# A rest computed in two halves on GpSimd, each half awaited by TensorE by itself

## The reference, cut to what matters

```python
e = emb_table[feat_index]                      # 512 x 39 x 16
x0 = e
h1 = relu(einsum('bhd,bmd,ohm->bod', x0, x0, conv_w1) + conv_b1)
nxt, hi1 = split(h1, 2, axis=1)                # 64 and 64 rows
h2 = relu(einsum('bhd,bmd,ohm->bod', nxt, x0, conv_w2) + conv_b2)
res = concatenate([hi1, h2], axis=1).sum(axis=2)
y = relu(_bn(flat @ deep_w1 + deep_b1, ...))   # 400 wide, statistics over the batch
y = relu(_bn(y @ deep_w2 + deep_b2, ...))
return concatenate([flat @ linear_w, res, y], axis=1) @ out_w + out_b
```

## Time and profile before

| | us |
|---|---|
| median of 3 runs | 464.21 (463.79 to 464.5) |
| the profiled execution | 464.01 |
| its span, first to last instruction | 462.2 |
| PE busy | 403.8 (87%) |
| DVE busy | 362.8 (79%) |
| POOL busy | 319.2 (69%) |
| ACT busy | 198.2 (43%) |

### The profile page before, as it was taken

The page is one execution under the profiler, slowest core; times in us unless marked ns, Lnnn a source line. Parts: engine busy times, 40 slices in busy tenths (PEclk is TensorE's granted clock), DMA queues, the critical chain, the costliest instruction groups (busy, mean ns, idle before and its releaser), DMA issues. The chain is left out here.

```text
span 462.2 us, 4571 instructions
## 1 busy us (share of the span) xinstructions
PE 403.8 (87%) x1238; PEld 229.4 (50%) x1238; DVE 362.8 (79%) x369; ACT 198.2 (43%) x252; POOL 319.2 (69%) x232
## 2 busy tenths in 40 slices
PE   0001959999999999999999999989999999979996
PEld 0001524554465555556555555546557565655563
DVE  6222658979958888999779777999874988998994
ACT  1104012327432751465156524734564447656443
POOL 5787777775848667886888878832478268729662
PEclk9999988999999999999999999999999999999999
DMA  3756959999998988899999979988957999998910
GB/s 64 146 85 146 152 63 244 238 171 210 221 235 186 226 205 192 191 228 243 237 209 215 219 183 206 232 227 212 220 128 186 236 230 236 241 258 213 237 38 2
DMA packets 41726, 87.95 MB, mean 190 GB/s; under 512 B 15836, under 2 KB 21275, under 8 KB 41700
## 3 DMA queue, kind: packets, MB, share of 16 engines
q1 hardware_dynamic: 28693, 80.48, 70.9%
q0 software_dynamic: 5120, 1.32, 7.9%
q10 hardware_dynamic: 7887, 5.86, 5.4%
HBM read 86.34 MB, written 1.28 MB: 190 GB/s over the span
## 5 line engine op out<-in xcount | busy, mean ns | idle before, releaser
L540 POOL TENSOR_TENSOR zl<-ring,zh 128x1024 fp32r<-128x1024 f32 x60 | 142.5, 2389 | 83.0 <-ACT zh L1022 78.9
L526 POOL DMA_INDIRECT G<-in_emb,idx_all x160 | 161.5, 1010 | 48.2 <-issue 41.7
L662 DVE TENSOR_TENSOR ring<-p_n,ring 128x1024 f32<-128x1024 f32 x147 | 174.0, 1217 | 0.9
L1022 ACT ACTIVATE zh<-ring 128x1024 fp32r<-128x1024 f32 x81 | 85.3, 1056 | 133.3 <-DVE ring L662 130.2
L833 PE MATMUL p_h<-ring,w2s 128*128 128x512 f32 x264 | 124.6, 602 | 6.3 <-DVE ring L662 5.4
L833 PE MATMUL p_n<-placed,w1s 125*128 125x512 f32 (+2 forms) x192 | 92.0, 603 | 0.0
L662 DVE TENSOR_TENSOR placed<-xa,p_x 125x1024 f32<-125x1024 f32 (+2 forms) x45 | 54.7, 1216 | 37.0 <-PE p_x L812 37.0
L833 PEld LDWEIGHTS p_h<-ring,w2s 128*128 128x128 f32 x264 | 50.6, 193 | 56.0 <-issue 44.3
L833 PE MATMUL p_h<-zh,w2l 128*128 128x512 f32 x178 | 68.2, 464 | 1.6 <-DVE zh L625 1.6
L812 PE MATMUL p_x<-stack,put 103*125 103x512 f32 (+3 forms) x116 | 52.5, 534 | 9.7 <-DVE stack L635 9.3
L833 PE MATMUL p_h<-zh,w2h 128*128 128x512 f32 x178 | 56.0, 396 | 0.0
(11 more groups left out here) (113 smaller groups left out, 303.0 us busy)
## 6 DMA issues: line engine op xcount, KB each, us to landing
ring<-xs_scratch SPq DMA_DIRECT2D x294, 256.0 KB, 5.6
xa<-xs_scratch ACTq DMA_DIRECT2D x21, 156.0 KB
G<-in_emb,idx_all POOLq DMA_INDIRECT x160
xs_scratch<-xT ACTq DMA_DIRECT2D x16, 64.0 KB
dw_sb<-in_dw SPq DMA_DIRECT2D x4, 200.0 KB
xa<-xs_scratch SPq DMA_DIRECT2D x3, 156.0 KB
xa<-in_dw ACTq DMA_DIRECT2D x2, 156.2 KB
xa<-xs_scratch ACTq DMA_DIRECT2D x7, 32.0 KB
```

The source lines that it names most:

```text
L526: nc.gpsimd.indirect_dma_start(G[:, b % 2, DIM * f:DIM * (f + 1)], None, emb[:, :], bass.IndirectOffsetOnAxis(idx_all[:, b, f:f + 1], 0)). ...
L540: nc.gpsimd.tensor_tensor(low_of(s), z_of(s), high_of(s).bitcast(F32), ALU.subtract).then_inc(s_low_pool, 1)
L662: nc.vector.tensor_tensor(z_of(s), by, x, ALU.mult).then_inc(s_z, 1)
L1022: nc.scalar.activation(high_of(s), z_of(s), ACT.Copy).then_inc(s_zh, 1)
```

## The change

In GpSimd's `low_part` the one subtraction over 1024 columns becomes two over 512 columns each, and each raises s_low_pool by one. The count that others wait for is therefore doubled (`wait_used`, and TensorE). TensorE waits for the first half ahead of its first matmul on zl, and for the second half ahead of its second. Rests by VectorE stay whole, with one wait.

```diff
@@ wait_used
             elif s in POOL_SPLITS:
-                own_wait(eng, s_low_pool, POOL_SPLITS.index(s) + 1)
+                own_wait(eng, s_low_pool, CHUNKS * (POOL_SPLITS.index(s) + 1))
@@ low_part on GpSimd
                 wait_low_room(pool, s)
                 own_wait(pool, s_zh, SPLITS.index(s) + 1)
-                nc.gpsimd.tensor_tensor(low_of(s), z_of(s), high_of(s).bitcast(F32), ALU.subtract).then_inc(s_low_pool, 1)
+                for c in range(CHUNKS):
+                    half = slice(BANK * c, BANK * (c + 1))
+                    nc.gpsimd.tensor_tensor(low_of(s)[:, half], z_of(s)[:, half], high_of(s)[:, half].bitcast(F32),
+                                            ALU.subtract).then_inc(s_low_pool, 1)
@@ contract on TensorE
-                    rest, count = (s_low_dve, DVE_SPLITS) if s in DVE_SPLITS else (s_low_pool, POOL_SPLITS)
+                    rest, count, parts = (s_low_dve, DVE_SPLITS, 1) if s in DVE_SPLITS else (s_low_pool, POOL_SPLITS, CHUNKS)
...
                         for c in range(CHUNKS):
                             mm(c, wh, high)
-                        pe.wait_ge(rest, count.index(s) + 1)
                         for c in range(CHUNKS):
+                            if c < parts:
+
+                                pe.wait_ge(rest, parts * count.index(s) + c + 1)
                             last = mm(c, wh, low, False, final)
```

## The result

Seven runs of the changed kernel have a median of 462.59 us (461.22 to 464.88), seven of the kernel before on the same chip 464.72 (463.79 to 465.63). The ratio is 0.9954, 95% interval 0.994 to 0.9968: faster by 0.46%, some 2.1 us. Forecast were 459.5 and -4.55 us. The sign was right and the time lies in the range, but the size was more than twice too large.

The account below looks back on a forecast made before the run. TensorE was taken as the bound, so gains could come only from its idle time. Terms of -0.25, -2.2, -1.1 and -1.0 sum to -4.55 us, from 464.01 to 459.5 us, range 458.5 to 463.6.

Parts of the forecast that it names:

- GpSimd's cost: Two halves cost 0.10 us more than one rest, 6.0 us over 60, hidden by GpSimd's 83.0 us of idle time.
- TensorE's 60 new waits: A second wait ahead of each pair's second matmul on zl, if already satisfied, costs 0, at most 0.01 us.
- VectorE is let in between halves: VectorE instructions held by a GpSimd rest go at the boundary between its halves; terms 2 to 4 build on it.
- Rival B: Nothing measurable: VectorE isn't let in between halves of one rest, only the direct halves' gain is left; 463.5 us, chance 0.14.
- C: Slower: the second wait keeps TensorE from loading weights under the first matmul, 0.10 us per rest; 465.5 us, chance 0.06.
- Term 1: TensorE's wait for a rest at 257.39: one matmul instead of two stands behind the last half; -0.25 us.
- Term 2: First normalisation chain: L722 and L732 wait for halves, shortening TensorE's waits at 410.55 and 415.72; -2.2 us.
- L722 goes at 403.53, so L732 is up at 404.53: Term 2's step: L722 goes behind the first half, the three small steps between take 0.95 us.
- Term 3: Block 4: the gather moves behind VectorE's L630, L625 at 299.86 is no longer held, TensorE's 1.18 wait goes; -1.1 us.
- Term 4: Last wait, 450.92: the half brings 0.25 directly and VectorE in front is earlier; -1.0 us, at best all 1.34.
- VectorE gains at least 0.5: Term 4's step: 1.1 gained at the second L732, at worst 0.6 lost at L630 at 428.61.
- Rival A: Only part comes: term 2 or 3 fails, term 4 at its low end; 460.8 or 461.9 us, chance 0.25.

Follow-up runs that it names:

- the small kernel: Computes nothing of the model: 32 stages, VectorE probes beside six GpSimd subtractions of 512 columns; six take 7.36 us with the tiny probe, 8.35 with the two-input one.
- one wait: Changed kernel, but TensorE waits once for both halves ahead of its first matmul on zl; 462.64 us against 464.95 before, ratio 0.9948.
- two rests: Kernel before with only the two GpSimd rests beside the first normalisation chain halved; 463.77 us against 464.95, ratio 0.9978.
- the PSUM version: Kernel before, whole rests, with the results of L722 and L732 written to PSUM instead of SBUF; second run 461.94 us against 465.25, ratio 0.9929.
- Blocks 1 to 4: Kernel before with only the 24 GpSimd rests of blocks 1 to 4 halved; 491.11 us against 491.17 on a slow-loading chip, ratio 0.9994.
- Halves with the exchange: Changed kernel with rest (7,9) moved to GpSimd and (7,11) to VectorE; 491.89 us against 491.17 on a slow-loading chip, ratio 0.9989.
- quarters: Changed kernel with each GpSimd rest in four pieces of 256 columns, TensorE waiting for the second and fourth; 473.01 us against 465.1 before, ratio 1.0178.
- with PSUM: Changed kernel with the results of L722 and L732 in PSUM, run twice; ratios against the kernel before 0.9924 and 0.9917 (460.84 us against 465.25).
- PSUM and the exchange: Changed kernel with L722's and L732's results in PSUM and rests (7,9) and (7,11) exchanged between VectorE and GpSimd; 463.38 us against 465.1 before, ratio 0.9956.

## Why the prediction was right or wrong

- *GpSimd's cost and TensorE's 60 new waits.* Right in size: 0.14 us per rest more (0.10 forecast), and a mean of 400 ns on zl. The cover held only behind block 4: before the change GpSimd had 2.4 us of idle time ahead of the rests between 260 and 306 us, and TensorE had lost 0.57 us by block 4's h2s. The Trainium skill's figure in "GPSIMD Engine Reference", "Performance pitfalls for Q7 kernels", gave an estimate of 0.17 for one more piece, a little nearer than mine. The page states it for a read command; two of them for a subtraction were my assumption. Two sums beside the main one were wrong: with 0.17 the first term is 0.35 - 0.17 = 0.18 and the sum -4.5, not -4.4, and all of terms 3 and 4 makes -4.97, not -5.1.
- *VectorE is let in between halves.* Right for the small steps and for most two-input instructions. Rival B is refuted by L735, let in at 405.91 between the halves of one rest, and by the small kernel; C by the mean on zl.
- **Term 1, -0.25.** Came to nothing (+0.04). One matmul less behind the wait is worth 0.22 (block 3's h2s is at +0.27 with one wait and at +0.05 with two), where I had put 0.35, and the rest itself is 0.25 later (one wait shows 0.56 for it where it was 0.31), by the halves' own 0.14 and what GpSimd has before it. I had taken off only 0.10.
- **Term 2, -2.2: the main miss, measured -1.25.** The step that failed is "L722 goes at 403.53, so L732 is up at 404.53". It left out that the square root between them waits for ScalarE's table load, which ended at 404.35, and it counted 1.55 and 0.84 of TensorE's waits as all VectorE's, while 0.87 of the first was ScalarE's h2s. Phase was bad luck on top and by the estimate above cost little: L725's turn came 0.05 behind a boundary. The second half of the term, L732 let in at a boundary, is right (1.1 us). That these rests alone give it was shown by two rests (-1.02); that the load is next, by two rests and by the PSUM version.
- **Term 3, -1.1, measured -0.9.** Mechanism and size right, in all seven profiles with halves there. Timelines of GpSimd and VectorE of the changed kernel:

```profile
293.76 1.76 POOL L526 DMA_INDIRECT G<-in_emb,idx_all  x1 [0.16 <-issue]
```
```profile
300.79 1.24 DVE L628 TENSOR_TENSOR zh<-placed,zh 64x1024 fp32r<-64x1024 f32 x1
```

  The gather fell behind VectorE's subtraction (293.12) and took 1.76, L628 took 1.24 where L625 took 3.92, and the wait is gone. But GpSimd reached this gather 0.8 us later than before, not 0.2. That fits the halves' costs adding up where there is little idle time, and isn't shown by a run of its own. The 0.35 at 305.57 is the price that I had called a trifle. Blocks 1 to 4 shows how little makes it a loss.
- **Term 4, -1.0, measured -0.25.** The step that failed is "VectorE gains at least 0.5". Timelines of VectorE and GpSimd of the changed kernel:

```profile
427.51 4.14 DVE L633 TENSOR_TENSOR zl<-ring,zh 128x1024 fp32r<-128x1024 f32 x1
```
```profile
415.64 14.93 POOL L542 TENSOR_TENSOR zl<-ring,zh 128x512 fp32r<-128x512 f32 x12 [8.48 <-ACT zh L1027]
```

  VectorE waited until all twelve halves were through (430.57), 14.93 us where the six rests took 14.08. From the stretch's start L633 ended 1.20 sooner than L630 had (431.65 - 119.69 against 431.95 - 118.79), while TensorE was by then some 2.0 sooner: VectorE lost 0.85 of its lead there, more than the 0.6 of my low bound, which counts a pair at 2.45 where my own cost says 2.49. L735's 1.1 of the second chain gave it back, and little more was left for the last wait, 0.27 + 0.75 against 1.34. Halves with the exchange, where the hand-overs were won, has no last wait and a stretch 1.5 us shorter.
- *The sum.* +0.04, -1.25, -0.9 and -0.25 make -2.36; small shifts elsewhere, +0.07 of them between the h2s of blocks 5 and 6, make up the rest to -2.23.
- *Rival A* is what came in number (its two cases are -3.2 and -2.1, measured were -2.1 timed and -2.2 in the stretch), but not as it was put, so that the match is luck: neither of terms 2 and 3 failed whole; three terms came short. The Trainium skill's rule that the first to issue holds the ports for its whole length ("SBUF — State Buffer", "Who interferes with whom") explains each hold up to the next boundary. It does not explain the row at 427.51, where VectorE stood ready before two halves began, and both went ahead of it, nor the row at 299.86 that the prediction had named.

**Open:** why a ready two-input instruction loses every boundary at (7, 9), or at (7, 10) after the exchange. In the last 260 us of the seven profiles with halves in four or more blocks, 20 two-input subtractions met a half with another directly behind it: 15 were let in at the first boundary, and five lost them all (4.14 us in the changed kernel, 3.91 with one wait, 4.16 and 4.13 with PSUM, 5.45 with PSUM and the exchange). Of the 15, 13 are the same two places in each profile, so this is fewer independent cases than it seems. With quarters the one at (7, 9) lost five boundaries, and one in block 6 lost one. Nor is it block 7 alone: in all five profiles with whole rests in block 4, VectorE's L625 at 299.86 started 0.48 ahead of a rest and still ended behind it (3.92 to 3.96 us). A gather's issue was under way beside it, but gathers at the same offset with no rest behind them held no VectorE instruction. I have no cause. Not tried: transfers, ScalarE's work or a long row of GpSimd pieces ahead of the small kernel's probes.

## What to carry to other kernels

When an engine's instruction takes longer than its kind, ask first whether its operand or its output can live elsewhere: here two small outputs in PSUM gave 3.1 and 3.3 us of stretch, and cutting 60 instructions of the other engine in two gave 2.2. When a stall is to go, write down what each engine behind it waits for next, table loads and freed accumulators too, before taking its whole length as gain. A cost on an engine with idle time is covered only where that idle time lies: read it by stage. A gain that rests on two engines' order within 0.05 us needs a discount, and pieces should be no smaller than the tightest stage can pay.

## What the runs showed of the hardware

- A GpSimd subtraction of 1024 columns takes 2.39 us, one of 512 1.26, and four of 256 in a row 2.79 to 2.84: halving costs 0.14 and quartering 0.4.
- A tiny VectorE tensor_scalar from SBUF to SBUF waits for the running GpSimd subtraction (1.53 and 1.41 us beside whole rests, 0.16 and 0.17 with its output in PSUM), costs GpSimd nothing, and ends 0.03 behind the boundary. A reciprocal from SBUF to SBUF beside a rest took 0.18. A two-input subtraction of 1024 columns ends 1.08 behind the boundary and pushes the next piece back by 1.0.
- GpSimd's issue of a gather is held by VectorE's two-input instruction as its subtractions are: 1.99 instead of 0.95 us when it comes 0.05 later. When it comes at most 0.03 later, or first, it takes 0.94 to 0.96.
- The same instruction at the same place, 1.89 us behind the same start, was let in at the first boundary in one profile and lost three in another.
